# A routed two-layer expert kernel: the hand-over from early to late pairs reordered on four engines

## The reference, cut to what matters

```python
x = x + xattn(layernorm(x), token_ids, ctx)      # expert of a token is given by its id, 4 experts
x = x + ffn(layernorm(x), G, gate_w, up_w, down_w, lora_A, lora_B)
# ffn:
scores = softmax(x @ G); value, indices = top_k(scores, 2)      # 8 experts, 2 for each token
gate, up = silu(x @ gate_w[e].T), x @ up_w[e].T                 # 64 wide
out = sum over the two experts of value * (gate * up @ down_w[e].T + (x @ lora_A[e].T) @ lora_B[e].T)
```

## Time and profile before

| | before |
|---|---|
| median of three runs | 303.4 us (302.93 to 304.19) |
| the profiled execution, its own time | 304.11 us |
| its span, first to last instruction | 302.1 us |
| mean granted TensorE clock | 0.96 of full |
| busy: PE, DVE, ACT, POOL | 263.3, 228.7, 151.1, 163.0 us |
| first late load issued by SP | 195.16 us |
| first transpose of late rows, tx(7) | 198.26 us |
| last store issued | 291.17 us |

### The profile page before, as it was taken

The page is one execution under the profiler, slowest core; times in us unless marked ns, Lnnn a source line. Parts: engine busy times, 40 slices in busy tenths (PEclk is TensorE's granted clock), DMA queues, the critical chain, the costliest instruction groups (busy, mean ns, idle before and its releaser), DMA issues. The chain is left out here.

```text
span 302.1 us, 6151 instructions
## 1 busy us (share of the span) xinstructions
PE 263.3 (87%) x1653; PEld 227.7 (75%) x1653; DVE 228.7 (76%) x701; ACT 151.1 (50%) x375; POOL 163.0 (54%) x159
## 2 busy tenths in 40 slices
PE   0658999999999999999999996679999999999900
PEld 0646788888878888888887795569999998999700
DVE  7686858768988878898898879937999976666500
ACT  3522334444454454444645264225666678888810
POOL 3668423353258834883048861724444448676760
PEclk9999999999999999999999999758999999999975
DMA  7562999810123212440004963398666659999830
GB/s 264 197 229 80 282 252 357 295 27 10 37 96 115 94 35 70 150 161 7 2 35 174 320 203 103 116 298 264 198 216 182 201 142 158 219 224 123 102 48 0
DMA packets 23279, 45.97 MB, mean 152 GB/s; under 512 B 4540, under 2 KB 8636, under 8 KB 22656
## 3 DMA queue, kind: packets, MB, share of 16 engines
q0 software_dynamic: 9488, 21.84, 27.4%
q1 hardware_dynamic: 13760, 23.74, 25.9%
HBM read 24.49 MB, written 25.80 MB: 166 GB/s over the span
## 5 line engine op out<-in xcount | busy, mean ns | idle before, releaser
L433 POOL DMA_INDIRECT out<-pair_out,dest_now x37 | 48.9, 1322 | 32.0 <-DVE pair_out L970 12.1
L511 ACT ACTIVATE aT_hi<-p_aT 128x512 fp32r<-128x512 f32 x19 | 11.3, 597 | 52.9 <-PE p_aT L1097 52.9
L1191 PE MATMUL p_y<-ctx_hi,aT_hi 128*128 x76 | 31.6, 416 | 0.0
L1191 PE MATMUL p_h<-ctx_hi,xT_hi 128*128 x72 | 29.9, 416 | 1.4 <-ACT xT_hi L507 1.4
L381 POOL DMA_INDIRECT xin<-x,gather_row x19 | 20.2, 1061 | 18.3 <-DVE rec L775 14.2
L1192 PE MATMUL p_y<-ctx_lo,aT_hi 128*128 x76 | 30.0, 395 | 0.0
L1192 PE MATMUL p_h<-ctx_lo,xT_hi 128*128 x72 | 28.4, 395 | 0.0
L388 POOL TENSOR_TENSOR rstd<-var_eps,neg_half 128x1 f32<-128x1 f32 x19 | 12.7, 668 | 27.2 <-DVE var_eps L744 27.0
L405 POOL DMA_INDIRECT rows_a<-rec,dest x19 | 18.9, 995 | 5.7 <-issue 5.7
L1283 PE MATMUL p_y<-down_hi,aT_hi 80*128 x44 | 21.7, 494 | 0.0
L405 POOL DMA_INDIRECT rows_b<-rec,dest x19 | 18.7, 982 | 5.5 <-issue 5.5
(11 more groups left out here) (278 smaller groups left out, 788.1 us busy)
## 6 DMA issues: line engine op xcount, KB each, us to landing
whole<-ctx_t SPq DMA_DIRECT2D x4, 1024.0 KB, 6.6
pair_x_late<-rows_b SPq DMA_DIRECT2D x13, 258.0 KB, 4.3
pair_x_early<-rows_a SPq DMA_DIRECT2D x10, 258.0 KB, 4.1
whole<-w_up SPq DMA_DIRECT2D x4, 576.0 KB, 6.9
rows_a<-pair_x_early SPq DMA_DIRECT2D x8, 258.0 KB, 11.3
rows_b<-pair_x_early SPq DMA_DIRECT2D x8, 258.0 KB, 11.8
pair_x_late<-rows_a SPq DMA_DIRECT2D x8, 258.0 KB, 4.0
pair_x_early<-rows_b SPq DMA_DIRECT2D x7, 258.0 KB, 3.5
```

Source lines behind the costliest of these rows:

```text
L433: nc.gpsimd.indirect_dma_start(out=out, out_offset=bass.IndirectOffsetOnAxis(ap=rows, axis=0), in_=pair_out[:, s % ORING, :], in_offset=No ...
L1191: nc.tensor.matmul(to, hi(i), w_hi(i), start=(i == 0), stop=False)
```

## The change

It has five parts.

- GpSimd: the three `scatter(t, 0)` of the last batch go ahead of `store(0)`, and the three `scatter(t, 1)` move up by one store each.
- The turn of the last tile (`turn_x2(18)`) goes ahead of `route(17)` on TensorE. For that, its copy on ScalarE is written into the buffer `act` instead of x2T, and is moved ahead of gate_silu(0).
- VectorE: `pair_gates` is cut in two, `exponents` and the rest. For the last batch both go ahead of `places`, and `take(1)` moves from behind gate_up(2) to ahead of lo2(2). The reduction of `exponents` gets a wait of its own. ScalarE's order follows (`put_stats` ahead of hi2(3), `route_exp` behind copy_b(2)).
- TensorE: `total` and `rank` of the last batch go ahead of up(3). Up(6), ta(5), down(4), ta(6) and down(5) go ahead of tx(7); then come tx(7), tx(8), up(7), tx(9), and the iterations from 8.
- VectorE and ScalarE follow this order: last_listed moves up to between al2(3) and gate_up(4), last_surplus behind lo2(6), pairs 5 and 6 are worked through ahead of lo2(7), last_limits stands between lo2(7) and lo2(8), and the iterations start from 7. The loop over `GROUPS` there finds no group that ends by pair 8.

```diff
@@ -212,6 +212,9 @@
 
         def x2_bank(t):
             return p_aT if t >= STEPS - 2 else p_x2T
+
+        def x2T_of(t):
+            return act if t == STEPS - 1 else x2T
 
         p_x, p_u, p_o = (p_xT, p_a), (p_h, p_x2T), (p_y, p_y1)
 
@@ -482,13 +485,12 @@
                 scatter(t, 1)
             inverse_deviation2(LAST)
             scatter(before_last[-1], 1)
-            store(0)
             for t in last:
                 scatter(t, 0)
-            for s in range(1, PAIRS):
+            for s in range(PAIRS):
                 store(s)
-                if 2 <= s < 2 + len(last):
-                    scatter(last[s - 2], 1)
+                if 1 <= s < 1 + len(last):
+                    scatter(last[s - 1], 1)
             for i in range(ORING):
                 pool.wait_ge(stored[i], 16 * ((PAIRS - i + ORING - 1) // ORING))
 
@@ -523,7 +525,7 @@
 
             def copy_x2T(t):
                 sc.wait_ge(x2T_ready, t + 1)
-                nc.scalar.activation(x2T[:], x2_bank(t)[:], ACT.Copy).then_inc(x2T_out, 1)
+                nc.scalar.activation(x2T_of(t)[:], x2_bank(t)[:], ACT.Copy).then_inc(x2T_out, 1)
 
             def copy_logits(t):
                 c = t % 2 * E2
@@ -627,22 +629,30 @@
             copy_b(0)
             copy_x2T(STEPS - 2)
             centre(STEPS - 1)
+            copy_x2T(STEPS - 1)
             gate_silu(0)
+            copy_logits(STEPS - 2)
             hi2(2)
-            copy_x2T(STEPS - 1)
-            copy_logits(STEPS - 2)
             copy_b(1)
             ah2(0)
+            copy_logits(STEPS - 1)
             gate_silu(1)
-            copy_logits(STEPS - 1)
+            put_stats(LAST)
             hi2(3)
             copy_b(2)
+            route_exp(LAST)
             ah2(1)
             gate_silu(2)
             hi2(4)
-            route_exp(LAST)
-            put_stats(LAST)
-            for i in range(3, PAIRS + 2):
+            for i in range(3, 5):
+                pair_iteration(i)
+            for i in range(5, 7):
+                copy_b(i)
+                ah2(i - 1)
+                gate_silu(i)
+            hi2(7)
+            hi2(8)
+            for i in range(7, PAIRS + 2):
                 pair_iteration(i)
 
         @block.vector
@@ -816,16 +826,19 @@
                 nc.vector.tensor_tensor(z[:, 0:n, :], z[:, 0:n, :], rstd2[:, ts].unsqueeze(2).broadcast_to([P, n, E2]),
                                         ALU.mult).then_inc(z_ready, 1)
 
-            def pair_gates(b):
-                t0, t1 = BATCHES[b]
-                n = t1 - t0
-                ts = slice(t0, t1)
+            def exponents(b):
+                n = BATCHES[b][1] - BATCHES[b][0]
                 dve.wait_ge(z_silu_ready, b + 1)
                 step(nc.vector.scalar_tensor_tensor(z_rest[:, 0:n, :], z[:, 0:n, :], -1.0, z_silu[:, 0:n, :],
                                                     ALU.add, ALU.subtract), route_step)
                 step(nc.vector.reciprocal(z_rest[:, 0:n, :], z_rest[:, 0:n, :]), route_step)
                 step(nc.vector.tensor_tensor(z_exp[:, 0:n, :], z_silu[:, 0:n, :], z_rest[:, 0:n, :], ALU.mult), route_step)
-                nc.vector.tensor_reduce(z_sum[:, 0:n], z_exp[:, 0:n, :], AX_X, ALU.add)
+                step(nc.vector.tensor_reduce(z_sum[:, 0:n], z_exp[:, 0:n, :], AX_X, ALU.add), route_step)
+
+            def pair_gates(b):
+                t0, t1 = BATCHES[b]
+                n = t1 - t0
+                ts = slice(t0, t1)
                 pairs = [P, n, 2, E2]
                 step(nc.vector.tensor_tensor(picked[:, 0:n], onehot[:, ts], z_exp[:, 0:n, :].unsqueeze(2).broadcast_to(pairs),
                                              ALU.mult), route_step)
@@ -1019,6 +1032,7 @@
                 for b, (t0, t1) in enumerate(BATCHES):
                     if k == t1 + 3:
                         places(b)
+                        exponents(b)
                         pair_gates(b)
                 if k == BATCHES[EARLY_BATCH[0]][1] + 4:
                     take(0)
@@ -1027,6 +1041,7 @@
                     if k == t1 + 2 and b < LAST - 1:
                         owners(b)
             places(LAST - 1)
+            exponents(LAST - 1)
             pair_gates(LAST - 1)
             early_list(1)
             residual(STEPS - 2)
@@ -1040,30 +1055,47 @@
             lo2(1)
             combine(0)
             gate_up(0)
+            take(1)
             lo2(2)
             choose(STEPS - 2)
             combine(1)
             al2(0)
+            choose(STEPS - 1)
             gate_up(1)
-            choose(STEPS - 1)
             owners(LAST)
             lo2(3)
             combine(2)
+            exponents(LAST)
             al2(1)
             gate_up(2)
-            take(1)
+            pair_gates(LAST)
+            places(LAST)
             lo2(4)
-            places(LAST)
             pair_finish(0)
-            pair_gates(LAST)
             pair_iteration(3)
             last_list()
-            pair_iteration(4)
+            combine(4)
+            al2(3)
             last_listed()
+            gate_up(4)
+            pair_finish(2)
+            lo2(6)
             last_surplus()
-            pair_iteration(5)
+            combine(5)
+            al2(4)
+            gate_up(5)
+            pair_finish(3)
+            combine(6)
+            al2(5)
+            gate_up(6)
+            pair_finish(4)
+            lo2(7)
             last_limits()
-            for i in range(6, PAIRS + 2):
+            lo2(8)
+            for group in GROUPS:
+                if group[-1] <= 8:
+                    take_dest(group)
+            for i in range(7, PAIRS + 2):
                 pair_iteration(i)
 
         @block.tensor
@@ -1116,7 +1148,7 @@
                 if t >= 1:
                     pe.wait_ge(logits_out, t)
                 for i in range(KB):
-                    last = nc.tensor.matmul(p_rt[:, c:c + E2], x2T[:, blk(i)], route_w[:, i * E2:(i + 1) * E2],
+                    last = nc.tensor.matmul(p_rt[:, c:c + E2], x2T_of(t)[:, blk(i)], route_w[:, i * E2:(i + 1) * E2],
                                             start=(i == 0), stop=(i == KB - 1))
                 last.then_inc(logits_ready, 1)
 
@@ -1333,8 +1365,8 @@
             turn_x2(STEPS - 2)
             tx(2)
             up(1)
+            turn_x2(STEPS - 1)
             route(STEPS - 2)
-            turn_x2(STEPS - 1)
             tx(3)
             ta(0)
             route(STEPS - 1)
@@ -1342,11 +1374,11 @@
             down(0)
             ta(1)
             tx(4)
-            up(3)
             total(LAST)
             rank(LAST)
+            up(3)
+            down(1)
             ta(2)
-            down(1)
             tx(5)
             up(4)
             ta(3)
@@ -1356,13 +1388,17 @@
             turn_list(2)
             ta(4)
             down(3)
-            tx(7)
             up(6)
-            spread_surplus()
             ta(5)
             down(4)
+            spread_surplus()
+            ta(6)
+            down(5)
+            tx(7)
             tx(8)
-            for i in range(7, PAIRS + 2):
+            up(7)
+            tx(9)
+            for i in range(8, PAIRS + 2):
                 pair_iteration(i)
```

## The result

The changed kernel takes 301.01 us (median of 20 runs, 298.87 to 304.88), the kernel before 303.23 us (20 runs on the same chip). The ratio is 0.9926, 95% interval 0.9908 to 0.9943: 2.2 us faster, where 5.4 were forecast. The ratio leaves out one run of the changed kernel, 304.88 us, that was over 1.5% above the fastest. The profiled execution has a span of 299.2 us against 302.1, that is 2.9 us less. The execution profiled before the change took 304.11 us, 0.9 above the median of 303.23, and the one after it 300.93, close to its median, so differences between the two traces are up to 1 us larger than the gain in the medians.

The account below looks back on a forecast made before the run. The start of TensorE's steady run, held by late rows and half clock, was taken to set the end. Gain 6.2 us at up(8), 5.8 by VectorE, less 0.4 for the clock: 303.4 - 5.4 = 298.0 us, range 296.7 to 301.8.

Parts of the forecast that it names:

- the prediction's own signs of being wrong: Wrong if: clock 0.5 from 198 to 206 again; last_list after 189.7; or a late pair's tx waiting for rows.
- Scatters, gates and places: GpSimd's first scatter at 187.1, last landing at 192.0; worth nothing by itself, as the list is already later.
- last_list at 189.5: VectorE: the earlier x2 turn and take(1) gain only 0.2 us; range ends 1.5 and -0.1.
- last_listed moved, 192.65 ready: VectorE: 1.5 us off between last_list and last_listed; `listed` ready at 192.65, first load 193.45, rows 196.5.
- TensorE at tx(7) by 197.65: TensorE does the moved work before the late rows, reaching tx(7) 0.6 us before the 198.26 of now.
- I take the end near 0: TensorE's clock cost, bounds 0 and 4.1 us of the gain: charged 0.4 us, for up(5) at half clock.
- rival 1: Half clock on TensorE's broken-up stretch until about 206, 301.7 us, or near 202.6, 300.0; chance 0.24 for both.
- tx(8) in between, its rows there at 198.6: TensorE: second late load issued 1.2 us after the first, 4.0 us to land, rows there before tx(8) needs them.
- rival 4: Late loads meet scatters and stores, take 5.2 us: tx(8), tx(9) 1.2 us later, 299.2 to 299.6; chance 0.12 with late scatters.
- 6.2 us at up(8): TensorE: up(8) at 200.55 against 206.79, with 4.85 us of work moved ahead of tx(7); VectorE's lo2(10) only 5.76 earlier.
- Steady run, end: TensorE's steady run unchanged at 2.19 us per pair, last matmul at about 282, the same 14.5 us behind it.
- The rival that ends slower: TensorE stays at half clock past 212.5: 305 us, or 306.7 if that lasted to 216; chance 0.06.

Follow-up runs that it names:

- experiment 1: Changed kernel plus short products, never read, in TensorE's holes, against the kernel before: 1.0111 on the first chip; 300.52 us, 0.9944 on the fourth.
- Experiment 4: Changed kernel with TensorE's order around the late rows put back, against the kernel before: 1.0016 on the first chip; 300.70 us, 0.9944 on the fourth.
- experiment 3: Kernel before with the last rows_a scatters ahead of store(0), then GpSimd waiting for pair 9's rows: 301.46 us, 0.9940 on the third chip.
- experiment 5: Changed kernel with last_listed put back behind lo2(6), against the kernel before: 1.0047 on the first chip; 300.92 us, 0.9965 on the fourth.
- experiment 2: Changed kernel, GpSimd waiting for pair 9's rows before store(0): 299.69 us, 0.9874, third chip; plus short products 298.33, 0.9840, and 298.56, 0.9870, fourth.

## Why the prediction came out as it did

The direction held, and the range by 0.8 us at its slow end; the size did not. Two of the prediction's own signs of being wrong came: a late pair's tx waited for its rows, and the clock was at 0.5, from 194 to 204 and not from 198 to 206. Step by step:

- **Scatters, gates and places: right.** First scatter forecast for 187.1, was at 186.61; the list, not the scatters, stayed last, by SP's 0.7 us wait.
- **last_list at 189.5: right,** it was 189.06, better by 0.4 us. **last_listed moved, 192.65 ready: right,** 192.14. First load 193.16 (forecast 193.45), its rows at 196.2 (196.5).
- **TensorE at tx(7) by 197.65: right for a full clock** (197.62 in experiment 1). At the half clock it was 198.46. ta(6) and down(5) did not wait for VectorE there.
- **"I take the end near 0" of the clock, 0.4 us: wrong in this execution.** No idle stretch was over 0.96 us, and the clock was still at 1.2 GHz from 194 to 204. Against the full clock of experiment 1 (up(8) at 202.26) that is 1.3 us of the 3.0 by which up(8) missed the forecast's 200.55; the two executions were not taken side by side. On the third chip the changed kernel's clock was at 1.2 GHz from 194 to 200.7, and with GpSimd held back it stayed full even without the short products, behind the same gaps and the same busy time (5.46 of 8 us against 5.48). So it is not a fixed cost, and what decides it in this stretch is open. The Trainium skill, page "TensorE: Matmul & The Clock Gate", section "HAM oscillation — how this bites in real kernels", describes a kernel whose waits for DMA between short bursts cost the clock. The trace shows such a loss too, ten us at 0.50, but after gaps of 0.96 us and shorter, while that section is about longer waits. The measured time lies in rival 1's band (300 to 301.9), which is luck: its path did not come about, with the list at 192.14 and not at 193.1 and tx(7) at 198.46 and not at 199.8. With the full clock alone no gain in time was seen (experiment 1).
- **"tx(8) in between, its rows there at 198.6": this is the step that failed.** I took 4.0 us for the second landing, the median of a row of the kernel before, and held it for hidden. It took 5.7 us (200.1), and it was the last thing to arrive for tx(8), and through it for up(7) and up(8). At full clock, with rows at 200.0, up(8) was at 202.26, so this step is 1.7 of the missing 3.0 us. I had looked at it as rival 4 but priced it at 1.2 us against a full sum. The earlier loads meet the rows_b scatters and stores more closely than before; with these held back the same landing fell from 5.0 to 2.9 us on the third chip and from 5.4 to 4.1 on the fourth. It does not bind in every execution: on the third chip the rows came at 199.28, and the half clock made TensorE just as late.
- **"6.2 us at up(8)", with 4.85 us of moved work in it: mis-sized by the same step.** The forecast, cut to 5.8 for VectorE and to 5.4 for the clock, stands against 3.24 us at up(8), and VectorE's lo2(10), which was to count, is at 207.06 against 209.92, 2.9 us. The rows of the second tile were there at 200.3 before and 200.1 after. Before, tx(8) came behind the work, at 202.69, and after, with the rows, at 200.21: 2.48 us were to be had, and not 4.85. Experiment 4 agrees: the old order did that work while the second tile was landing, so it was not free time given back as long as that landing stays last. The idle time that the change fills at tx(7) partly comes back as the 0.69 us at tx(8) and as half clock.
- **The two conditions together bring up(8) to the forecast's place.** With the second landing at 3.7 and 4.1 us, near the 4.0 that I took, and the full clock, the gain was 5.2 us on the third chip and 3.9 on the fourth. Not all of this is the change's: the hold alone made the old order 2.0 us faster (experiment 3). Holding GpSimd back was worth 2.0 us where the clock was full in both kernels. What the clock is worth once the rows come soon is not shown: 299.69 to 298.33 us has overlapping intervals, and in both profiles the clock was full; up(6) already came 0.84 us earlier in the second.
- **Steady run, end: right.** 2.19 us per pair from up(9) on, 14.5 us behind the last product.

The rival that ends slower did not happen by its mechanism (half clock past 212.5), yet on the second chip the changed kernel was slower than before, by a mechanism that I had not thought of: the stops in last_listed and hi2(7). What makes the engines stop is open. It is not shown that GpSimd's traffic does it: the kernel with GpSimd held back was run only on chips without such stops. The DMA records of the changed kernel on the second chip also hold instruction packets. Some lie beside stops (two in the half us from 169.0, VectorE resumes at 170.34; one in that from 209.5, ScalarE resumes at 211.05), but none lies between 155 and 169, where both engines stop up to 162.8, and none between 197 and 201.87, the stop of last_listed. The Trainium skill, page "Runtime: NRT & Kernel Launch", section "Instruction fetch mechanics", says that going over the end of a block of instructions is mostly hidden; these runs neither show nor refute that for last_listed.

## What to carry to other kernels

When a change lets the first of several loads go earlier, work out the second and third as well, with the landing time that they will have beside the traffic they now meet, and take the slowest row for them. Work moved into a hole is worth only what it stops hiding: ask what ran under it in its old place. GpSimd's stores and scatters that nobody reads soon can be held back by one wait until the loads on the path have landed.

## What the runs showed of the hardware that was not expected

- The second late load, 258 KB, took 2.9 to 4.1 us to land with GpSimd held back and 5.0 to 5.7 us, issued at 194.0 to 194.6, with scatters and stores in flight; issued at 195.62, beside them too, it took 3.9 (experiment 5). The first late load does not follow this: 2.6, 4.1 and 4.6 us held back, 2.9 to 3.5 otherwise. The issue of seven loads took 6.93 to 7.79 us held back and 7.86 to 8.47 in the other versions of the changed kernel, all on chips without stops.
- TensorE's clock went to 1.2 GHz at 194 with no idle stretch over 0.96 us in the preceding 8 us, of which it was busy 5.48, and the full clock came back after ten us. With the same gaps and 5.46 us busy it stayed full in the held-back kernel (experiment 2).
- The same kernel before has medians from 302.47 to 309.28 us on four chips, and on two of them VectorE stops for up to 3.5 us at a time, and ScalarE with it, at several places for which the profile shows no wait.
